# Grouping attention by output batch, with four operand buffers and the division by the softmax sums on GpSimd

## What is computed

```python
q = _lin(_lin(x, wq_w, wq_b), vq_w, vq_b)      # k and v alike
q = q.reshape(b, s, hc, H).transpose(2, 0, 1, 3)   # hc = 32 heads of H = 16
scores = jnp.einsum('cbqh,cbkh->cbqk', q, k) / scale
attn = jax.nn.softmax(scores, axis=-1)
o = jnp.einsum('cbqk,cbkh->cbqh', attn, v)
o = o.reshape(H, b, s, hc).transpose(1, 2, 0, 3).reshape(b, s, f)
return _lin(o, wo_w, wo_b)
```

## Time and profile before

| | us |
|---|---|
| median of 3 runs | 2444.63 (2431.52 to 2447.24) |
| the profiled execution | 2437.11 |
| its span, first to last instruction | 2435.2 |
| TensorE busy | 2224.9 (91%) |
| VectorE busy | 1731.4 (71%) |
| ScalarE busy | 1366.1 (56%) |
| GpSimd busy | 431.3 (18%) |

### The profile page before, as it was taken

The page is one execution under the profiler, slowest core; times in us unless marked ns, Lnnn a source line. Parts: engine busy times, 40 slices in busy tenths (PEclk is TensorE's granted clock), DMA queues, the critical chain, the costliest instruction groups (busy, mean ns, idle before and its releaser), DMA issues. The chain is left out here.

```text
span 2435.2 us, 41882 instructions
## 1 busy us (share of the span) xinstructions
PE 2224.9 (91%) x11688; PEld 1266.7 (52%) x11688; DVE 1731.4 (71%) x1806; ACT 1366.1 (56%) x2470; POOL 431.3 (18%) x814
## 2 busy tenths in 40 slices
PE   8999965999999999999999999999974989989896
PEld 4788852444444444444444444444413767766673
DVE  3333327898898899989988988989804665757565
ACT  0111201777777777777777777777742544444343
POOL 0000000000000000000000000000003575666664
PEclk9899985999999999999999999999967999999898
DMA  4244431222222222222222222222106544535341
GB/s 143 104 155 172 148 98 57 46 68 62 64 58 61 67 63 63 61 58 66 66 63 61 60 61 66 63 64 59 42 24 210 175 146 130 190 116 169 108 134 48
DMA packets 174858, 223.42 MB, mean 92 GB/s; under 512 B 93264, under 2 KB 94288, under 8 KB 168656
## 3 DMA queue, kind: packets, MB, share of 16 engines
q1 hardware_dynamic: 174800, 222.70, 31.5%
HBM read 169.12 MB, written 51.38 MB: 91 GB/s over the span
## 5 line engine op out<-in xcount | busy, mean ns | idle before, releaser
L476 DVE TENSOR_REDUCE neg_max<-psum 128x1 f32<-128x1024 f32 x1024 | 1203.6, 1219 | 167.1 <-PE psum L372 165.7
L456 ACT ACTIVATE probs<-psum 128x512 f32<-128x512 f32 x2048 | 1058.1, 602 | 419.7 <-PE psum L391 419.5
L391 PE MATMUL psum<-q_op,k_op 50*128 50x512 f32 x2048 | 757.9, 455 | 45.0 <-DMA k_op<-qk_parts_dram 31.6
L391 PEld LDWEIGHTS psum<-q_op,k_op 50*128 50x128 f32 x2048 | 351.3, 195 | 625.5 <-ACT probs L456 554.3
L372 PE MATMUL psum<-k_op,q_op 48*128 48x512 f32 x2048 | 637.8, 501 | 36.5 <-DMA k_op<-qk_parts_dram 26.6
L400 PE MATMUL psum<-probs,v_op 128*32 128x512 f32 x4096 | 562.3, 622 | 0.0
L372 PEld LDWEIGHTS psum<-k_op,q_op 48*128 48x128 f32 x2048 | 382.8, 315 | 86.3 <-DVE neg_max L476 42.1
L523 POOL CAST neg_max_parts<-neg_max 128x8 fp32r<-128x8 f32 x128 | 24.3, 189 | 1258.6 <-DVE neg_max L476 1258.6
L147 PE MATMUL psum<-x_hi,conv_w_hi 128*128 128x512 f32 x512 | 209.8, 410 | 6.9 <-DVE x_lo L1143 6.9
L147 PE MATMUL psum<-x_lo,conv_w_hi 128*128 128x512 f32 x512 | 204.2, 399 | 0.0
L147 PE MATMUL psum<-x_hi,conv_w_lo 128*128 128x512 f32 x512 | 204.2, 399 | 0.0
(11 more groups left out here) (96 smaller groups left out, 1812.6 us busy)
## 6 DMA issues: line engine op xcount, KB each, us to landing
qk_parts_dram<-qk_parts SPq DMA_DIRECT2D x64, 512.0 KB, 2.8
q_op<-qk_parts_dram SPq DMA_DIRECT2D x128, 256.0 KB
conv_w_raw<-in_conv_w_dram SPq DMA_DIRECT2D x64, 512.0 KB, 3.4
k_op<-qk_parts_dram SPq DMA_DIRECT2D x384, 64.0 KB
q_op<-qk_parts_dram SPq DMA_DIRECT2D x128, 128.0 KB
gate_in<-in_ctx_dram SPq DMA_DIRECT2D x64, 256.0 KB, 3.6
x_block<-in_x_t_dram SPq DMA_DIRECT2D x8, 1024.0 KB, 5.9
q_op<-neg_max_parts SPq DMA_DIRECT2D x512, 4.0 KB, 2.3
```

The costliest lines, as they stand in the source:

```text
L391: nc.tensor.matmul(s2_bank[cell % RING], kop[lo][r, b, n // 2 * P:(n // 2 + 1) * P], qop[lo][r, b, j % 2 * HALF:(j % 2 + 1) * HALF], start ...
L456: nc.scalar.activation(probs[n % DEEP][:, j, :], s2_bank[cell % RING], ACT.Exp, scale=SCALE).then_inc(exp_done, 1)
L476: nc.vector.tensor_reduce(mx[b][:, t:t + 1], s1_bank[t % 2][:], AX_X, ALU.max, negate=True).then_inc(maxed, 1)
```

## The change

Attention is regrouped so that one output batch is finished before the next begins. The 64 slots are now numbered by output batch (16 slots each), and the weights are permuted on loading so that heads of one parity stand together.

- `project` stores each part by a DMA of its own, three for each tile, in the row order in which `attend` reads it (a row block of 48 rows for each slot, the part needed twice is stored twice). Each has the shape 8 x 16 x 512. The values are written slot by slot.
- `attend` has four operand buffers of one slot each. `load_op` has four DMAs of 48 rows. The load for slot s+3 is issued at the start of slot s and first needed in the middle of slot s+1. The maxima are 24 units ahead (LEAD) instead of 32; the second half of a slot's maxima is taken in the first half of the slot before it. The copy of the value bank stays on VectorE, between maxima.
- The output of a slot is stored by one DMA (`store_out`). For every two slots SP loads the sums and the outputs back (`load_pair`), VectorE takes reciprocals of 128 x 32 (`recips`), SP stores them and loads them spread out (`load_recips`), GpSimd divides and splits (`normalise`: two 128 x 512 operations with two inputs and one copy), and SP stores both parts (`store_parts`).
- `wo` is loaded and split at the end of `attend`, and the first batch's parts are loaded there (`load_o`, two DMAs for each of eight chunks). The last pair is left to `finish`.
- In `finish` the divisions, `hi_o` and `lo_o` are gone from VectorE and ScalarE; `turn` loads the parts of batch b+1 straight into place, four DMAs after group 2 of each m.

The core of the diff:

```diff
 def project
...
-                            sp.dma_start(
-                                qk_scr[j // KC, :, (j % KC) * P:(j % KC + 1) * P, bass.ds(it * (2 * HALF) + i * HALF, HALF)]
-                                .rearrange("a f n -> f a n"), parts[j % 4][:].bitcast(F32)).then_inc(stored[j % 4], DMA)
...
+                        rows = qk_scr[j // KC, slot0 * ROWS:(slot0 + P // DH) * ROWS, cols]\
+                            .rearrange("(s r d) n -> s r d n", r=3, d=DH)
+
+                        sp.wait_ge(qk_lo, blk * (2 * KC) + j + 9)
+                        for r, part in enumerate((0, 0, 1) if j < KC else (0, 1, 0)):
+                            sp.dma_start(rows[:, r, :, :], parts[j % 4][:, part, :].bitcast(F32))\
+                                .then_inc(stored[j % 4], DMA)
...
-                for i in range(4):
-                    sp.wait_ge(stored[i], DMA * (BLK * 2 + 1))
+                    sp.wait_ge(stored[i], 3 * DMA * (BLK * 2) + DMA)
...
+    LEAD = 3 * QT
...
+        qop = [sb(f"q_op{i}", [P, 2, S], F32R) for i in range(4)]
+        kop = [sb(f"k_op{i}", [P, 2, HALF], F32R) for i in range(4)]
...
+        def load_op(sp, i, s):
+            q = qk_scr[0, bass.ds(s * ROWS, ROWS), :].rearrange("r (b n) -> r b n", b=2)
+            k = qk_scr[1, bass.ds(s * ROWS, ROWS), :].rearrange("r (b l n) -> r b l n", b=2, l=2)
             for lane in range(2):
...
+                rows = slice(LANE * lane, LANE * lane + ROWS)
+                sp.dma_start(qop[i][rows, :, :].bitcast(F32), q).then_inc(op_in[i], DMA)
+                sp.dma_start(kop[i][rows, :, :].bitcast(F32), k[:, :, lane, :]).then_inc(op_in[i], DMA)
...
+                def slot(it, k, first=False, last=False):
+                    s = it * 4 + k
...
+                        sp.wait_ge(s2_full, s * (STEPS * TILES))
+                        sp.sem_inc(waited, 1)
+                        load_op(sp, (k + 3) % 4, s + 3)
+                    if not (last and k == 3):
+
+                        sp.wait_ge(split, s * 2 + 3)
+                        store_max(sp, (k + 1) % 4, 0)
+                    if k % 2 == 0 and not first:
+                        store_parts(sp, norm, on_scr, it * 2 + (k - 4) // 2)
+                    if not (first and k == 0):
+
+                        sp.wait_ge(pv_out, s + 1)
+                        sp.sem_inc(waited, 1)
+                        store_out(sp, norm, us_scr, s - 1, (k - 1) % 2)
+                    if k % 2 == 0 and not (first and k == 0):
+                        load_pair(sp, norm, us_scr, it * 2 + (k - 2) // 2)
+                    if k % 2 == 1 and not (first and k == 1):
+                        load_recips(sp, norm, r_scr, it * 2 + (k - 3) // 2)
+                    if not (last and k == 3):
+                        sp.wait_ge(split, s * 2 + 4)
+                        store_max(sp, (k + 1) % 4, 1)
...
+def load_o(sp, late, on_scr, b, n):
+
+    i, c = n // KC, n % KC
+    for part, dst in enumerate((late["o_hi"], late["o_lo"])):
+        src = on_scr[part].rearrange("(h l q) n -> h l q n", l=2, q=VW)[bass.ds(b * 16 + c * 4, 4), i, :, :]
+        sp.dma_start(dst[:, n, :].bitcast(F32), src).then_inc(late["o_in"][i], DMA)
...
-                            if g == 2 and m < KC - 1 and not last:
-                                for n in (2 * m + 2, 2 * m + 3):
-                                    next_o(b + 1, n)
+                            if g == 2 and not last:
+                                for n in (2 * m, 2 * m + 1):
+                                    load_o(sp, late, on_scr, b + 1, n)
...
-                            if g == 1 and not last:
-                                for j in range(2):
-                                    divide(b + 1, 2 * m + j)
```

531 lines of the change are left out of this document (262 added, 269 removed).

## The result

| | before | now |
|---|---|---|
| median, us (4 runs each) | 2440.62 (2431.52 to 2447.24) | 2627.77 (2614.45 to 2633.24) |
| the profiled execution | 2437.11 | 2626.32 |
| its span | 2435.2 | 2624.6 |

A forecast was written before the change was run, and what follows sets the result against it. The prediction took TensorE's own stream as the bound. Its terms, 13 - 31 - 44 + 0 - 7 - 12 - 6 + 15 = -72, took 2437.1 to 2365 us profiled; it named 2370, range 2330 to 2410.

The forecast's parts named there:

- Start of attention: Lead of attention: faster first load -16, 24 units ahead instead of 32 -9.0, no 6.7 us maxima wait; -31 us.
- Borders of slots: Attention slots: operand loads issued earlier, without L308's two-engine tail, end border stalls; -42, with first four slots -44 us.
- What is added to a slot: Attention slots: added reciprocals, GpSimd work, stores and loads stay hidden in the engines' free time; 0 us.
- Rivals B and C: Attention: B, second-half maxima late, border stall moves, 2412, chance 0.06; C, SP's chain late every slot, 2445 to 2460, chance 0.03.
- Projection stores: Projection: stores with outer dimension 8 run on 8 engines, making a block 35.2 against 33.9 us; +13 us.
- the first of the two readings weighed in the prediction: DMA engine counts: a DMA's shape sets how many engines it gets, projection's stores 8 and `load_o` 4; gives the -72.
- Rival A: Projection: eight engines may not keep 24.2 GB/s each while x loads read; +43, 2395 to 2400 us, chance 0.10.
- The slack of today's stores: End of projection before the change: last store issued 12.5 us before the last product, read as ending at 349.3.
- wo of batches 1 to 3: `finish`: four `load_o` behind a weight load, on 4 engines, come some 5 us late, three times; +15 us.
- turns: Turns 0 to 2 of `finish`: divisions, high and low parts leave VectorE and ScalarE, shortening waits; -6 us.
- start of finish: Last attention copy to convolution: divisions and low parts leave VectorE, the wait for x and a little go; -12 us.
- Tail: End of attention: scores made ahead half a slot less, so less TensorE idle and three fewer slow steps; -7 us.

## Why the prediction was wrong

- **Start of attention (-31, measured -26.5): right in its parts.** The lead is 26.5 us instead of 42.5, as worked out (9 us of units and the 6.7 us wait). The first unit comes 8.8 us after the first issue (400.18 to 408.98), not 6, and from the last product to that issue it is 7.2 us instead of 4.8.
- **Borders of slots (-44, measured -41 without the fifteen long slots): right**, in cause too, by the run that splits L308 in the kernel before. The step outside the long slots stayed at 2.61 us, as forecast.
- **What is added to a slot (0): failed.** It costed what each engine has to do and never asked what each engine has to be given to do it: where its code stands. That the loop on ScalarE now holds the first four slots was in the diff, and taken for nothing. It cost 154.3 us, 59% of the 261 between forecast and result: in place of 0 the runs show a stop of ScalarE for its code at each of fifteen branches back, 7.7 us each, and TensorE's half clock behind it. Rivals B and C looked for a slower kernel in the right stretch, but put it in every slot and on SP; SP's second-half stores left 11.9 us into slot 13 (750.56), near the 8 to 11 estimated. The 0.2 us of the reciprocals in every second slot is a second, small miss of this step.
- **Projection stores (+13, measured +49.4): the mechanism half right, the size wrong.** Eight engines is right (0.53 of 16 at 205 GB/s), and so is four for `load_o` (0.26 at 102), as the first of the two readings weighed in the prediction had it. The sum added x's 2.7 us to the stores as if both could run without a break; the term that was missing is the 8 us in which VectorE waits for x behind the stores, and its split. Rival A's +43 came near by number, with the wrong reason: an engine does not make less than in the earlier trace rows, it makes 25.6 GB/s and stands idle in between. The slack of today's stores was also read too large: the last product ends at 346.5, so it is 9.7 us and not 12.5.
- **wo of batches 1 to 3 (+15, measured +47), turns (-6, measured +22), start of finish (-12, measured +1.6): failed by one step.** Each `load_o` was priced by its own time on 4 engines, right at 10.8 us for four. What stands behind it on these engines was not: weights, x and sums, and through the weights SP's own order, which then issued the last loads 19 us into the stage. Nor was SP, which the sixteen loads at the end of attention hold for 36.6 us; that most of them "can start in the last slots" did not help, the first left at 1920.3 and the last at 1954.4, 19 us after the last product. The work that left `finish` did pay, as the run with 128 rows shows: -36 us in `finish` against before, more than the 18 forecast for both terms, 29 of it at its start.
- **Tail (-7, measured -14.7): right in its sign, outside its ends (0 and -12).** From the first to the last score of the last slot it is 19.4 us at full clock in this run, against 29.95 before; in the other kernels with the same tail it took 19.4 to 30. So up to 10 us of this term turn on the clock of the run, and its size is in part luck.
- Sum of the misses: 154 in the loop, 36 in the projection, 74 in `finish`, less some 3 in the rest: 261. Without the first of them it would have been near 2472 us, still slower than before: the two steps on DMAs alone turn the forecast gain into a small loss.

## What to carry to other kernels

When a diff changes what is written out ahead of a loop, count the instructions of each engine's body and where it begins: the same body can be free in one place and cost 10 us a turn in another, and the sign is "issue" in front of the first instruction after the branch, on an engine that others wait for, together with transfers in the instruction queue. Price a DMA not only by its own time but by what stands behind it on the same engines and whom that feeds, and look whether the engine that issues it is held up; a load behind a burst of stores is late even where throughput suffices. Put a burst of transfers away from the moment at which the loops turn.

## What was not expected of the hardware

- 8 instructions ahead of a loop of 290 are worth 154 us in fifteen turns (2633 us with 128, 2628 with none, 2476 with 8), and transfers of code in queue 14 are 8 KB each, five a turn when the body doesn't fit. The same five a turn for SP's code (266 instructions) cost nothing.
- A transfer of code waits for data: from ScalarE's last register instruction to its next one it is 3.3 to 7.0 us with 1.2 MB issued at the same time, 2.0 to 2.2 us with the load some 9.5 us later.
- Eight DMA engines moved 205 GB/s of 2 KB pieces, 25.6 each, and four moved 102, 25.5 each, more than the 24.2 each of all 16 in a window of before.
- A row of sixteen loads on four engines holds up SP, which issues them: the first took 0.6 to 0.8 us, most of the later ones 2.5 us each, 36.6 in all, against 9.3 for the same sixteen on 128 rows.
- After a stop of 9 us on TensorE its clock is at 0.50 for 7 to 17 us, with steps of 4.07 us instead of 2.61; that is 47 of the 154 us which the long slots lose.
